# Rebuilding one of four attention stages of a vision tower: rotary attention with a transposed projection of image pairs

## The chip, the cores and the metric

One core of one Trainium2 chip (trn2). The metric is the device time of the kernel in microseconds (us), median of the runs; lower is better.

## The reference

The kernel is a small vision tower: a deformable-convolution tokenizer turns 32 images of 3x84x84 into 25 tokens of 192 numbers each, and four attention layers and four feed-forward layers follow, each with its residual and a layer norm behind it. The change touches the first attention layer alone. For x of 32 x 25 x 192 it computes

```python
# 12 heads of 16; LATENT = 32, so with n = 25 tokens ctx = n - LATENT = -7
ctx = n - LATENT
q, kv = _rope(_heads(x @ Wq)), _rope(_heads(x @ Wkv))     # kv serves as key and value
q = q * 16 ** (-0.5)
lkv, lkv_ctx = _ln(kv, ln_g, ln_b), _ln(kv[:, :ctx], ln_g, ln_b)   # layer norm of each head's 16 numbers
attn_lat = softmax(q[:, ctx:] @ kv.T)                    # the last 7 tokens attend to all 25
attn_ctx = softmax(q[:, :ctx] @ kv[:, :ctx].T)           # the first 18 only to the first 18
out_lat = _merge(attn_lat @ lkv) @ Wo_lat + bo_lat
out_ctx = _merge(attn_ctx @ lkv_ctx) @ Wo_ctx + bo_ctx
h = _layernorm(h + concatenate([out_ctx, out_lat], axis=1))
# _rope(t): t * cos(f) + concatenate([-t2, t1]) * sin(f), t1 and t2 the halves of a head's 16
```

## The kernel before

Tokens live in SBUF as `tw.y`, 8 tiles of 128 rows (TILES = 8). A tile holds 4 images (IMG_PER_TILE) of 25 tokens, each image padded to 32 rows (QUAD). The 12 heads go in 3 groups of 4 (GROUPS). The 192 features are contracted in two halves of 96 rows (HALVES, HALF). All is float32.

The program is a row of nine stages, one after the other: tokenizer, then attention and feed-forward of layers 0 to 3. Within a stage each engine has its own program, written out in the order in which it executes, and semaphores tie the engines together. No scheduler reorders anything. Stage 1, the rotary attention, is `softmax_attention` with kind "rope", opened by `AttentionBuffers`, whose block clears the buffers. It goes tile by tile in three steps of a software pipeline, `step(a, t, u, p)`: tile a is projected, tile t gets its scores, tile u is finished. On each engine:

- PE transposes the tokens (L258), projects q and kv of one tile token-major (L304: the transposed tokens are the stationary operand, 384 weight columns stream), transposes q and k head by head (L272, L274), makes the scores (L318), transposes the probabilities (L250), mixes the values (L287), transposes the result (L325) and multiplies it with both output matrices side by side (L332, 384 columns).
- DVE (VectorE) rotates (L349 to L352), centres kv and takes its variance (L355 to L360), scales it and applies the norm's gain and shift (L374 to L378), copies half of the keys (L431) and all values in 16 small copies (L440), divides by the softmax sum (L446, L448), adds the mask (L472), subtracts the maximum (L475, L477), and picks context or latent output row by row (L491, L494).
- ACT (ScalarE) copies transposed tiles out of PSUM, and makes Sqrt (L536) and Exp (L539) once per tile.
- POOL (GpSimd) adds the output bias (L552).

The layer norm is only begun here: `bn_stats` (L499) feeds a later part of the stage.

Two other attention stages, "unit" (stage 5) and "biased" (stage 7), already run through another function, `attention` (L557 on), which works on pairs of tiles. Its lines serve for comparison: it projects with the weights stationary and 200 token columns of two tiles streaming (L657), values as 64 small products per tile (L699), scores in 24 (L718), transposed probabilities (L727), the mix of the values (L739), the result transposed (L748), the output matrix in two halves (L756, L757); DVE spreads keys over four heads with a mask (L814), and divides (L859, L863). Stages 3 and 4 call the same pieces; L1298 is DVE's product of a projected bank of 400 columns with a table, in stage 3.

A float32 matmul of the code stands in the trace as two PE instructions, a transpose as one: the 12 products of L318 are the "x24" of a row.

## Time and profile before

| | us |
|---|---|
| median of 3 runs | 1305.06 (1305.06, 1314.97, 1294.93) |
| profiled execution, its own time | 1296.84 |
| its span | 1295.2 |
| PE busy in the span | 916.5 (71%) |
| DVE busy | 634.8 (49%) |
| ACT busy | 426.7 (33%) |
| stage 1, from the clearing of its buffers to the last of its `bn_stats` | 268.74 to 408.88 |

The profiled execution is the one whose rows are read below; its time lies 1.6 us above its span. A busy share is an average over nine stages with different limits, so the stage itself has to be read. Its three runs lie 20 us apart.

### The profile page before, as it was taken

To read this page: it belongs to the slowest core of one execution; us is meant where nothing else is said; L and a number is where in the kernel's file an instruction comes from. 1 tells how busy PE (TensorE), PEld (TensorE's weight loads), DVE (VectorE), ACT (ScalarE), POOL (GpSimd) and SP (SyncE) were. 2 spreads that over 40 slices of the span, in tenths; PEclk is the share of its full clock that TensorE was granted. 3 is DMA by queue.
4 is the path that set the end of the run, shared out by engine and by line. 5 is a ranking of instruction groups with operands and counts; after the bars stand their busy time and mean duration, and the time that the engine had idled before them with its cause. 6 is when DMAs were issued, how large, how long until landed. Compare 5 with 4: busy or idle time off the path is not lost. (4 is left out here: it accounts for less than half of the span.)

```text
span 1295.2 us, 25468 instructions
## 1 busy us (share of the span) xinstructions
PE 916.5 (71%) x9931; PEld 748.1 (58%) x9931; DVE 634.8 (49%) x1464; ACT 426.7 (33%) x728; POOL 214.8 (17%) x240
## 2 busy tenths in 40 slices
PE   4946677736766299358887658578778999386684
PEld 1336676423334199347776557366547999364573
DVE  1638899448774531365553225635281111246354
ACT  0148999123342112024443213334210112133132
POOL 2122232010000333142220010100002331200100
PEclk9969999855555599778998659868586999769598
DMA  4367787661000655100000060000053995100000
GB/s 126 80 135 182 191 205 196 175 156 25 0 0 1 217 142 129 60 1 2 2 2 1 2 163 4 2 2 3 2 133 80 238 258 124 32 2 3 1 4 20
DMA packets 63203, 100.35 MB, mean 77 GB/s; under 512 B 15812, under 2 KB 47096, under 8 KB 63104
## 3 DMA queue, kind: packets, MB, share of 16 engines
q1 hardware_dynamic: 57600, 93.25, 28.5%
q0 software_dynamic: 5504, 5.70, 2.1%
q8 instruction: 72, 1.18, 0.4%
q14 instruction: 27, 0.22, 0.1%
HBM read 91.34 MB, written 8.12 MB: 77 GB/s over the span
## 5 line engine op out<-in xcount | busy, mean ns | idle before, releaser
L1751 PE MATMUL ps_rows<-stage_strip,stage_hat_y 128*128 128x144 f32 x800 | 110.8, 295 | 53.2 <-ACT stage_hat_y L1718 53.2
L1751 PEld LDWEIGHTS ps_rows<-stage_strip,stage_hat_y 128*128 128x128 f32 x800 | 102.3, 193 | 61.8 <-ACT stage_hat_y L1718 36.5
L1782 DVE TENSOR_TENSOR stage_product<-ps_rows,stage_hat_x 128x1296 f32<-128x1296 f32 x80 | 68.7, 901 | 24.4 <-PE ps_rows L1751 23.7
L2558 DVE TENSOR_TENSOR L_ffnhid<-L_ffnact_gate,L_ffnbank_u 128x300 f32<-128x300 f32 x32 | 14.9, 467 | 119.0 <-ACT L_ffnact_gate L2576 119.0
L1790 DVE TENSOR_REDUCE stage_samples<-stage_product 128x1440 f32 x40 | 66.2, 1654 | 9.3 <-DVE stage_product L1782 9.3
L1733 POOL TENSOR_TENSOR stage_hat_x<-stage_pos_xT,stage_w_window_x 128x240 f32<-128x240 f32 x80 | 48.3, 625 | 108.7 <-DVE stage_product L1782 102.6
L1713 ACT ACTIVATE stage_hat_y<-stage_hat_y,stage_w_minus_row 80x1280 f32<-80x1280 f32 x40 | 54.4, 1361 | 26.9 <-DMA stage_hat_y<-places_y 26.4
L1556 PE MATMUL ps_conv<-stage_w_offset_w,stage_patches 128*100 128x512 f32 x96 | 44.0, 611 | 17.2 <-DMA stage_patches<-in_patchesT 17.2
L1718 ACT ACTIVATE stage_hat_y<-stage_hat_y 80x1280 f32<-80x1280 f32 x40 | 50.1, 1253 | 0.0
L1135 PE MATMUL L_attnbank_q<-L_attnhT,L_attnwq 97*128 97x200 f32 x192 | 43.2, 372 | 6.9 <-DVE L_attnqT L1298 6.7
L1135 PEld LDWEIGHTS L_attnbank_q<-L_attnhT,L_attnwq 97*128 97x128 f32 x192 | 36.7, 212 | 9.4 <-issue 8.7
L2522 PE MATMUL L_ffnbank_g<-L_ffnxT,L_ffn_win 96*128 96x100 f32 x240 | 41.0, 299 | 0.5 <-ACT L_ffnxT L2569 0.5
L2522 PE MATMUL L_ffnbank_u<-L_ffnxT,L_ffn_win 96*128 96x100 f32 x240 | 40.7, 297 | 0.0
L2491 POOL DMA_INDIRECT stage_y_rows<-L_ffndown,stage_choice_index x16 | 25.5, 1593 | 90.4 <-ACT L_ffndown L2583 90.4
L2576 ACT ACTIVATE L_ffnact_gate<-L_ffnbank_g 128x300 f32<-128x300 f32 x32 | 13.4, 420 | 80.5 <-PE L_ffnbank_u L2522 74.9
L1556 PEld LDWEIGHTS ps_conv<-stage_w_offset_w,stage_patches 128*100 128x100 f32 x96 | 16.0, 173 | 39.8 <-issue 22.6
L2342 DVE TENSOR_TENSOR L_ffnhid<-L_ffnact_gate,L_ffnbank_u 128x480 f32<-128x480 f32 x16 | 10.5, 654 | 55.6 <-ACT L_ffnact_gate L2366 50.4
L1174 PE MATMUL L_attnbank_o<-L_attnv_heads,L_attnwork 128*100 128x68 f32 x192 | 26.2, 314 | 16.1 <-ACT L_attnwork L1422 14.9
L2522 PEld LDWEIGHTS L_ffnbank_g<-L_ffnxT,L_ffn_win 96*128 96x128 f32 x240 | 36.0, 215 | 0.8 <-issue 0.8
L2522 PEld LDWEIGHTS L_ffnbank_u<-L_ffnxT,L_ffn_win 96*128 96x128 f32 x240 | 35.6, 213 | 0.0
L1174 PEld LDWEIGHTS L_attnbank_o<-L_attnv_heads,L_attnwork 128*100 128x100 f32 x192 | 25.0, 226 | 18.1 <-ACT L_attnwork L1422 16.0
L2290 PE MATMUL L_ffnbank_g<-L_ffnxT,L_ffn_win 96*128 96x240 f32 x128 | 33.0, 383 | 0.7 <-ACT L_ffnxT L2359 0.7
(430 smaller groups left out, 2197.6 us busy)
## 6 DMA issues: line engine op xcount, KB each, us to landing
stage_hat_y<-places_y SPq DMA_DIRECT2D x40, 400.0 KB
stage_strip<-in_strips SPq DMA_DIRECT2D x40, 315.0 KB
L_ffn_win<-in_L_ffn_Win SPq DMA_DIRECT2D x10, 1152.0 KB
stage_L_ffn_win<-in_L_ffn_Win SPq DMA_DIRECT2D x6, 1152.0 KB
L_ffnranks<-stage_ranks SPq DMA_DIRECT2D x16, 400.0 KB
L_ffn_win<-in_L_ffn_Win SPq DMA_DIRECT2D x8, 768.0 KB
L_ffn_wout<-in_L_ffn_Wout SPq DMA_DIRECT2D x10, 576.0 KB
stage_L_ffn_wout<-in_L_ffn_Wout SPq DMA_DIRECT2D x6, 576.0 KB
```

Of the source, the lines that this page charges most:

```text
L1135: mm = nc.tensor.matmul(bank_q[:, i * PAIR_TOKENS:(i + 1) * PAIR_TOKENS], wq[0:rows, k, c * GROUPS + g, :], tokens, start=(k == 0), stop=( ...
L1174: mm = nc.tensor.matmul(bank_o[0:QUERIES, j // 2, at:at + OUT_COLS], work[:, t % 2, j * GROUPS + g, :], v_heads[:, t % 4, j, g, :, :], sta ...
L1556: mm = nc.tensor.matmul(ps_conv[0:TILE_TOKENS, p, :], patches[:, p, c, :], w["offset_w"][:, c, :], start=(c == 0), stop=(c == SLABS - 1))
L1713: nc.scalar.activation(y, y, ACT.Abs, bias=w["minus_row"][0:ROWS_Y, :]).then_inc(s["hat_y_abs"], 1)
L1718: nc.scalar.activation(y, y, ACT.Relu, scale=-1.0, bias=1.0).then_inc(s["hat_y"], 1)
L1733: x = nc.gpsimd.tensor_tensor(hat_x[:, p, h * GRID * IMG_PER_TILE:(h + 1) * GRID * IMG_PER_TILE, :].rearrange("q (g j) x -> q g j x", j=IM ...
L1751: mm = nc.tensor.matmul(ps[:, p % 2, bank, at * cols:(at + 1) * cols], hat_y[:, p, g, h * P:(h + 1) * P], rhs.rearrange("q j c x -> q (j c ...
L1782: last = nc.vector.tensor_tensor(split(product[:, p % 2, slots.start * cols:slots.stop * cols]), ps[:, p % 2, banks, 0:used * cols].rearra ...
L1790: nc.vector.tensor_reduce(into.rearrange("q h c w -> q h w c"), by_window, AX_X, ALU.add).then_inc(s["summed"], 1)
L2290: mm = nc.tensor.matmul(ps[:, c, f, :], weights.win[e % NB][:, k, o:o + P], xT[:, e % 2, k, :], start=(k == 0), stop=(k == 1))
L2491: nc.gpsimd.indirect_dma_start(choice.y_rows, bass.IndirectOffsetOnAxis(choice.index[0:C, e:e + 1], 0), down[:, e % RING, :], None, bounds ...
L2522: mm = nc.tensor.matmul(ps[:, c, f, :], weights.win[e % NB][:, k, o:o + P], xT[:, e % 2, k, :], start=(k == 0), stop=(k == 1))
```

## The change

`AttentionBuffers` and `softmax_attention` go, `rope_attention` takes their place, with prepared weights: copies of Wq and Wkv whose two halves of each head are swapped, cos and sin tables by feature row, a centring matrix, the mask as two vectors whose outer product it is, and the output matrices with their biases as a 97th row. Apart from it, `build` and `layout` change only in what they load. The core of the diff:

```diff
-        w1 = halves("L0_attn_Wqkv", pending), halves("L0_attn_Wo", pending), tw.sb("w_L0_attn_bo", [P, DIM])
...
+        rope = {"qk": weight("w_L0_attn_qk", ins["L0_attn_qk"], [HALF, HALVES, 3, 2, P], pending),
+                "proj": weight("w_L0_attn_proj", ins["L0_attn_proj"], [PADDED_ROWS, 2, HALVES, DIM], pending),
+                "cos_sin": weight("w_rope_cos_sin", ins["rope_cos_sin"], [P, 2, TOKENS], pending), "centre": weight("w_rope_centre", ins["rope_centre"], [P, 4, 2 * HEAD_DIM], pending),
...
-            b = AttentionBuffers(tw)
-            softmax_attention(tw, b, "L0_attn", "rope", *w1, rope=rope, fetch=lambda sp: weights2.load(sp, range(4)))
+            rope_attention(tw, "L0_attn", rope, lambda sp: weights2.load(sp, range(4)))
```

PE's new functions (f counts pairs of tiles, t tiles; `bank_of` is bank_b for FIRST_K and LAST, bank_a for FIRST_Q):

```diff
+            def project(f, b):
+                pe.wait_ge(hT_ready, 2 * f + 2)
+                if b == LAST:
+                    pe.wait_ge(turned[FIRST_K], f + 1)
+                elif f:
+                    pe.wait_ge(turned[FIRST_Q if b == FIRST_Q else LAST], f)
+                for turn in range(2):
+                    for k in range(HALVES):
+                        tokens = hT[:, f % 2, k].rearrange("q z (j n) -> q (z j) n", n=QUAD)[:, :, 0:TOKENS]
+                        mm = nc.tensor.matmul(bank_of[b][:, turn * PAIR_TOKENS:(turn + 1) * PAIR_TOKENS], w["qk"][0:HALF, k, b, turn, :], tokens,
+                                              start=(k == 0), stop=(k == 1))
+                mm.then_inc(in_psum[b], 1)
+
+            def project_values(t):
+                f, z = t // 2, t % 2
+                pe.wait_ge(rotated[FIRST_K], f + 1)
+                pe.wait_ge(rotated[LAST], f + 1)
+                if t:
+                    pe.wait_ge(v_ready, t)
+                for j in range(IMG_PER_TILE):
+                    image = z * IMG_PER_TILE + j
+                    for a in range(4):
+                        to = ps_v[QUAD * a:QUAD * (a + 1), GROUPS * j:GROUPS * (j + 1), :].rearrange("n g d -> n (g d)")
+                        nc.tensor.matmul(to[:, 0:2 * HEAD_DIM], kr[:, f % 2, 0, image, :], w["centre"][:, a, :], start=True, stop=True)
+                        mm = nc.tensor.matmul(to[:, 2 * HEAD_DIM:], kr[half:P, f % 2, 1, image, :], w["centre"][half:P, a, HEAD_DIM:], start=True, stop=True)
+                mm.then_inc(v_in_psum, 1)
...
+                for g in range(GROUPS):
+                    rows = slice(half, P) if g == 1 else slice(0, half)
+                    nc.tensor.matmul(bank_s[:, g, 0:4 * TOKENS], w["context"][0:1, :], w["latent"][0:1, :], start=True, stop=False)
+                    for j in range(IMG_PER_TILE):
+                        mm = nc.tensor.matmul(bank_s[QUAD * j:QUAD * (j + 1), g, 0:4 * TOKENS], qT[rows, f % 2, g // 2, z * IMG_PER_TILE + j, :],
+                                              kd[rows, f % 2, g // 2, z * IMG_PER_TILE + j, :, :], start=False, stop=True)
...
+                for c in range(2):
+                    for k, rows in enumerate((HALF + 1, HALF)):
+                        mm = nc.tensor.matmul(ps_y, outT[0:rows, t % 2, c, k].rearrange("q j n -> q (j n)"), w["proj"][0:rows, c, k, :],
+                                              start=(c == 0 and k == 0), stop=(c == 1 and k == 1))
...
+            for i in range(-2, TILES + 2):
+                f, z = i // 2 + 1, i % 2
+                ahead = f < PAIRS
+                if 0 <= i < TILES:
+                    score(i)
+                if 1 <= i <= TILES:
+                    turn_probs(i - 1)
+                if ahead and z == 0:
+                    project(f, FIRST_K)
+                    project(f, FIRST_Q)
+                if 1 <= i <= TILES:
+                    mix_values(i - 1)
+                if i >= 2:
+                    turn_out(i - 2)
+                if ahead and z == 0:
+                    project(f, LAST)
+                if 0 <= i + 1 < TILES:
+                    project_values(i + 1)
+                if f + 1 < PAIRS:
+                    turn_tokens(2 * f + 2 + z)
+                if i >= 2:
+                    project_out(i - 2)
```

DVE's order, and its new pieces:

```diff
+            def turn(f, b):
...
+                nc.vector.tensor_tensor(pair(parts[:, f % 2, b].rearrange("p s n -> p (s n)")), pair(bank_of[b][:, 0:2 * PAIR_TOKENS]),
+                                        w["cos_sin"][:].unsqueeze(2).to_broadcast([P, 2, IMAGES_2, TOKENS]), ALU.mult).then_inc(turned[b], 1)
...
+            def store_values(t):
+                dve.wait_ge(v_inverse, t + 1)
...
+                for a in range(4):
+                    rows = slice(QUAD * a, QUAD * (a + 1))
+                    last = nc.vector.tensor_tensor(v_heads[rows, t % 4, :, :, a, 0:HEAD_DIM].rearrange("p j g d -> p (j g) d"), ps_v[rows],
+                                                   v_rstd[rows, t % 2, :].unsqueeze(2).to_broadcast([QUAD, IMG_PER_TILE * GROUPS, HEAD_DIM]), ALU.mult)
+                last.then_inc(v_ready, 1)
...
+            for i in range(-2, TILES + 2):
...
+                if 0 <= i < TILES:
+                    shift(i)
+                if 0 <= i < TILES:
+                    sum_values(i)
+                if 1 <= i <= TILES:
+                    divide(i - 1)
+                if ahead and z == 0:
+                    turn(f, FIRST_K)
+                    turn(f, FIRST_Q)
+                if ahead and z == 1:
+                    spread_last_keys(f)
...
+                    rows = w["proj"][0:HALF].rearrange("q c k n -> q (c k n)")
+                    nc.vector.tensor_scalar(rows, rows, w["gain"][:], None, ALU.mult).then_inc(scaled_out, 2)
+                if 0 <= i < TILES:
+                    store_values(i)
+                if ahead and z == 0:
+                    turn(f, LAST)
+                if i >= 2:
+                    add_residual(i - 2)
```

ACT makes the values' squares and their inverse deviation (Ln, then Exp), and POOL the sums of the two products of a rotation:

```diff
+                nc.scalar.activation(v_square[:], bank_h[:, 0:v_cols], ACT.Square).then_inc(v_squared, 1)
...
+                nc.scalar.activation(v_rstd[:, t % 2, :], v_rstd[:, t % 2, :], ACT.Ln, scale=1.0 / HEAD_DIM, bias=tw.eps[:]).then_inc(v_logged, 1)
+                act.wait_ge(v_logged, t + 1)
+                nc.scalar.activation(v_rstd[:, t % 2, :], v_rstd[:, t % 2, :], ACT.Exp, scale=-0.5).then_inc(v_inverse, 1)
...
+            for f in range(PAIRS):
+                pool.wait_ge(turned[FIRST_K], f + 1)
...
+                add(everything, kr, f, FIRST_K).then_inc(rotated[FIRST_K], 1)
...
+                add(everything, qT, f, FIRST_Q).then_inc(rotated[FIRST_Q], 1)
...
+                nc.gpsimd.tensor_tensor(kd[:, f % 2, 0], kr[:, f % 2, 0, :, 0:TOKENS].unsqueeze(2).to_broadcast(shape),
+                                        w["head_mask"][:].unsqueeze(1).unsqueeze(3).to_broadcast(shape), ALU.mult).then_inc(k_wide, 1)
...
+                add(low, qT, f, LAST).then_inc(last_q_rotated, 1)
...
+                add(high, kr, f, LAST).then_inc(rotated[LAST], 1)
```

What stands in a row now. PE, one step of the loop before (stage_probs of the tile being finished, stage_qk of the one in the middle):

```order
L250 MATMUL L_attnps_kT<-identity,stage_probs 128x128 x3
L258 MATMUL L_attnbank_h<-identity,stage_h 96x128 x2
L272 MATMUL L_attnps_qT<-identity,stage_qk 128x128 x3
L274 MATMUL L_attnps_kT<-identity,stage_qk 128x128 x3
L287 MATMUL L_attnps_o<-stage_v_heads,stage_pT 32x68 x12
L304 MATMUL L_attnps_qk<-w_L_attn_Wqkv,stage_hT 128x384 x2
L318 MATMUL L_attnps_s<-stage_kT,stage_qT 32x100 x12
L325 MATMUL L_attnbank_o<-identity,stage_out 96x128 x2
L332 MATMUL L_attnbank_v<-w_L_attn_Wo,stage_outT 128x384 x2
```

PE in the changed kernel, the even step i = 2, from its last group of scores on (bank_b twice: keys, then LAST; the pair L226, L227 stands 16 times, of which two are shown):

```order
L252 MATMUL L_attnbank_t<-identity,L_attnprobs 128x128 x3
L212 MATMUL L_attnbank_b<-L_attnhT,w_L_attn_qk 128x200 x4
L212 MATMUL L_attnbank_a<-L_attnhT,w_L_attn_qk 128x200 x4
L263 MATMUL L_attnbank_o<-L_attnv_heads,L_attnpT 32x68 x12
L272 MATMUL L_attnbank_t<-identity,L_attnout 96x128 x2
L212 MATMUL L_attnbank_b<-L_attnhT,w_L_attn_qk 128x200 x4
L226 MATMUL L_attnbank_h<-w_rope_centre,L_attnkr 32x32
L227 MATMUL L_attnbank_h<-w_rope_centre,L_attnkr 32x16
L226 MATMUL L_attnbank_h<-w_rope_centre,L_attnkr 32x32
L227 MATMUL L_attnbank_h<-w_rope_centre,L_attnkr 32x16
```

The six transposes of queries and keys are gone, the projection comes once for two tiles, and 32 small products for the values are new. In an odd step the three rows of L212 are absent, so the values' products come right behind L263 and L272.

DVE in the changed kernel, the odd step i = 3:

```order
L366 TENSOR_REDUCE L_attntop<-L_attnbank_s 128x12
L370 TENSOR_TENSOR L_attnprobs<-L_attnbank_s,L_attntop 128x12x25
L344 TENSOR_REDUCE L_attnv_rstd<-L_attnv_square 128x12
L375 RECIPROCAL L_attninv_sum<-L_attnbank_o 128x12
L379 TENSOR_TENSOR L_attnout<-L_attnbank_o,L_attninv_sum 128x192
L337 TENSOR_TENSOR L_attnkd<-L_attnkr,w_rope_head_mask 64x800
L353 TENSOR_TENSOR L_attnv_heads<-L_attnbank_h,L_attnv_rstd 32x12x16 x4
L384 TENSOR_TENSOR y<-L_attnbank_o,y 128x192
L386 BN_STATS moments<-y 128x6
```

`store_values` (L353) stands behind `divide` and `spread_last_keys` (L337), and the values' products of the next tile, on PE, wait for it.

## Rows read from the trace of the kernel before

**Rows 1.** Windows: stages 1, 5, 7: busy PE, PEld, DVE, ACT, POOL, PEclk, DMA, GB/s.

```profile
267.20:411.35 144.15, 85.24 (x552) 47.12 (x552) 99.29 (x344) 44.13 (x80) 8.20 (x10) 0.55 0.13 33
833.10:925.70 92.60, 65.22 (x1056) 51.22 (x1056) 44.30 (x108) 29.75 (x75) 10.81 (x8) 0.65 0.01 2
1126.60:1196.60 70.00, 49.68 (x1032) 39.02 (x1032) 38.77 (x93) 22.71 (x55) 4.67 (x4) 0.77 0.01 2
```

**Rows 2.** Timeline of stage 1: its clearing, first scores and last operation.

```profile
268.74 1.46 POOL L191 MEMSET stage_v_heads<- 128x1632 f32 x1 [30.09 <-POOLq L83]
...
290.37 0.72 PE L318 MATMUL L_attnps_s<-stage_kT,stage_qT 128*32 128x100 f32 x24
...
408.52 0.36 DVE L499 BATCH_NORM_STATS2 moments<-y 128x6 f32<-128x192 f32 x1
```

**Rows 3.** Costliest DVE group of stage 1, by shape.

```profile
L440 DVE COPY stage_v_heads<-stage_v 32x48 f32<-32x48 f32 x128 | 23.5, 183 | 1.9
```

**Rows 4.** Windows: three pair periods and the tail of the unit stage.

```profile
856.70:872.70 16.00, 12.42 (x225) 10.30 (x226) 7.27 (x17) 5.62 (x15) 1.53 (x1) 0.68 0.01 2
872.70:887.70 15.00, 12.37 (x269) 10.25 (x270) 8.58 (x22) 6.70 (x18) 1.54 (x1) 0.88 0.01 3
887.70:904.00 16.30, 13.34 (x264) 10.78 (x265) 8.61 (x22) 6.02 (x17) 1.53 (x1) 0.80 0.01 2
904.00:923.80 19.80, 15.17 (x153) 10.11 (x153) 7.07 (x20) 3.67 (x10) 0.00 (x0) 0.51 0.00 1
```

**Rows 5.** Timeline of the unit stage at half clock: PE, and DVE's reciprocal.

```profile
857.53 1.70 PE L657 MATMUL L_attnbank_b<-L_attnhT,w_L_attn_qk 97*128 97x200 f32 x4
...
861.83 1.59 PE L699 MATMUL L_attnbank_h<-w_L_attn_v,L_attnhT 97*32 97x51 f32 x64
...
887.67 0.89 PE L718 MATMUL L_attnbank_s<-L_attnkd,L_attnqT 64*32 64x100 f32 x24 [1.54 <-DVE L_attnkd L814]
888.49 0.90 PE L727 MATMUL L_attnbank_t<-identity,L_attnprobs 128*128 128x128 f32 x3
...
893.32 0.91 PE L739 MATMUL L_attnbank_o<-L_attnv_heads,L_attnpT 128*32 128x68 f32 x24
894.30 0.23 DVE L859 RECIPROCAL L_attninv_sum<-L_attnbank_o 128x12 f32<-128x12 f32 x1 [4.71 <-PE L_attnbank_o L739]
...
907.88 1.01 PE L756 MATMUL L_attnbank_o<-w_L_attn_proj,L_attnoutT 97*128 97x192 f32 x2 [0.46 <-ACT L_attnoutT L959]
908.69 0.85 PE L757 MATMUL L_attnbank_o<-w_L_attn_proj,L_attnoutT 96*128 96x192 f32 x2
```

**Rows 6.** The same at full clock, with ACT's copy of the probabilities.

```profile
895.41 0.59 PE L756 MATMUL L_attnbank_o<-w_L_attn_proj,L_attnoutT 97*128 97x192 f32 x2
...
896.26 0.55 PE L718 MATMUL L_attnbank_s<-L_attnkd,L_attnqT 64*32 64x100 f32 x24
896.74 0.55 PE L727 MATMUL L_attnbank_t<-identity,L_attnprobs 128*128 128x128 f32 x3
897.12 0.84 PE L683 MATMUL L_attnbank_h<-L_attnsquare,w_same_head 128*128 128x200 f32 x4
897.33 0.48 ACT L952 COPY L_attnpT<-L_attnbank_t 128x384 f32<-128x384 f32 x1 [1.11 <-PE L_attnbank_t L727]
898.24 0.56 PE L739 MATMUL L_attnbank_o<-L_attnv_heads,L_attnpT 128*32 128x68 f32 x24
898.87 0.23 DVE L859 RECIPROCAL L_attninv_sum<-L_attnbank_o 128x12 f32<-128x12 f32 x1 [0.87 <-PE L_attnbank_o L739]
```

**Rows 7.** Source lines: min/median/max ns of one, from first to last, shapes.

```profile
L1298 DVE TENSOR_TENSOR L_attnqT<-L_attnbank_q,w_cheb_q x24: 567/574/578, 571.1 to 695.8; 128x400 f32<-128x400 f32 x24
L814 DVE TENSOR_TENSOR L_attnkd<-L_attnk_unit,w_head_mask x4: 1366/1368/1375, 855.2 to 902.5; 64x800 f32<-64x800 f32 x4
L552 POOL TENSOR_TENSOR stage_resid<-stage_h,w_L_attn_bo x8: 587/588/592, 276.1 to 390.3; 128x192 f32<-128x192 f32 x8
L863 DVE TENSOR_TENSOR L_attnout<-L_attnbank_o,L_attninv_sum x16: 356/357/358, 867.9 to 1190.7; 128x192 f32<-128x192 f32 x16
```

More of the change, by code:

```diff
@@ L542, in _, with store_tokens, square_values @@
-            tiles(act, step)
+            def store_tokens(t):
+                act.wait_ge(hT_in_psum, t + 1)
+                f, z = t // 2, t % 2
+                if f >= 2:
+                    act.wait_ge(in_psum[LAST], f - 1)
+                    act.wait_ge(in_psum[FIRST_Q], f - 1)
+                nc.scalar.copy(hT[:, f % 2, :, z, :], ps_hT.rearrange("q (k n) -> q k n", n=P)).then_inc(hT_ready, 1)
+            def square_values(t):
+                act.wait_ge(v_in_psum, t + 1)
+                if t:
+                    act.wait_ge(v_summed, t)
+                nc.scalar.activation(v_square[:], bank_h[:, 0:v_cols], ACT.Square).then_inc(v_squared, 1)
@@ new lines, in store_probs, with store_out @@
+            def store_probs(t):
+                act.wait_ge(pT_in_psum, t + 1)
+                if t >= 2:
+                    act.wait_ge(out_in_psum, t - 1)
+                nc.scalar.copy(pT[:, t % 2].rearrange("p g n -> p (g n)"), bank_t[:, 0:GROUPS * P]).then_inc(pT_ready, 1)
+            def store_out(t):
+                act.wait_ge(outT_in_psum, t + 1)
+                act.wait_ge(ones_ready, 1)
+                if t >= 2:
+                    act.wait_ge(y_in_psum, t - 1)
+                for c, kind in enumerate(KINDS):
+                    last = nc.scalar.copy(outT[0:HALF, t % 2, c, :, :, kind], ps_outT.rearrange("q (k j n) -> q k j n", k=HALVES, n=QUAD)[:, :, :, kind])
+                last.then_inc(outT_ready, 1)
@@ new lines, in _ @@
+            nc.scalar.preload_act_table_set("natural_log_exp_and_others")
+            store_tokens(0)
+            store_tokens(1)
+            for i in range(-2, TILES + 2):
+                f, z = i // 2 + 1, i % 2
+                if 0 <= i < TILES:
+                    square_values(i)
+                if 1 <= i <= TILES:
+                    store_probs(i - 1)
+                if 0 <= i < TILES:
+                    exponent(i)
+                    invert_values(i)
+                if i >= 2:
+                    store_out(i - 2)
+                if f + 1 < PAIRS:
+                    store_tokens(2 * f + 2 + z)
@@ L544, in _ @@
         @block.gpsimd
         def _(pool):
[L546 to L554 removed]
+            nc.gpsimd.memset(outT[:], 0.0).then_inc(out_cleared, 1)
+            nc.gpsimd.memset(kr[:], 0.0).then_inc(qk_cleared, 1)
@@ new lines, in _, with add @@
+            nc.gpsimd.memset(qT[:], 0.0).then_inc(qk_cleared, 1)
+            nc.gpsimd.memset(probs[:], 0.0).then_inc(probs_cleared, 1)
+            nc.gpsimd.memset(v_heads[:], 0.0).then_inc(v_cleared, 1)
+            pool.wait_ge(qk_cleared, 2)
+            def add(rows, to, f, b):
+                p = parts[rows, f % 2, b]
+                return nc.gpsimd.tensor_tensor(to[rows, f % 2, b // 2, :, 0:TOKENS], by_image(p[:, 0, :]), by_image(p[:, 1, :]), ALU.add)
+            everything, low, high = slice(0, P), slice(0, half), slice(half, P)
@@ L2970, in with_bias @@
         return np.stack([np.concatenate([weight[:HALF], ends[0]]), np.concatenate([weight[HALF:], ends[1]])], 1)
+    o["L0_attn_proj"] = np.stack([with_bias(a[x], a[y]) for x, y in rope_proj], 1)
     def heads_first(x):
```

587 lines of the change are left out of this document (207 added, 380 removed).

## The prediction

> **What bounds the kernel now.** I first read the busy time by stage [rows 1]. In stage 1 (first row, 144.15 us with the norm behind it) VectorE, DVE, is busy 99.29 us in 344 operations and PE 85.24 us: neither is full, and they take turns. The other two rows are attention stages of the same size whose program resembles the new one. They take 92.60 and 70.00 us, with DVE busy 44.30 and 38.77 us. So the old stage is long because of DVE's many operations. The largest group of them is the 128 small value copies, 23.5 us [rows 3].
>
> The timeline shows what can be won [rows 2]: clearing begins at 268.74, the first scores start at 290.37 and the last statistics at 408.52. That is 118.15 us for eight tiles, 14.8 us each; a part of it is the drain behind the last scores. I count a pair of tiles as 30.8 us before. Nothing outside this stretch changes but weight loads, which come long before their use and lie beside the tokenizer's 268 us; I count them at nothing. If they were late the stage would start later, by microseconds, which the range holds.
>
> The last thing to see is the granted TensorE clock: 0.55 in the old stage, 0.65 and 0.77 in the other two [rows 1]. The clock has two levels, 2.4 GHz (1.0) and 1.2 GHz (0.5). Within the unit stage it is 0.68, 0.88 and 0.80 in three pair periods and 0.51 in the tail [rows 4]. Every PE duration therefore needs two prices.
>
> **The prices.** At half clock [rows 5]: twelve instructions of 200 columns fill 857.53 to 861.83, 0.36 us each; 24 score instructions 0.82 (887.67 to 888.49); two output instructions of 192 columns 0.81 (907.88 to 908.69); from mix to DVE's reciprocal 0.98; 64 value instructions 1.59. At full clock [rows 6]: scores 0.48, probability transposes 0.38, output instructions 0.85 for four, mix to reciprocal 0.63. From the transposes' start to the mix it is 1.17: 0.59 until ACT's copy starts, its 0.48 and 0.1 of hand-over; at half clock 0.3 more. 200 columns at full clock: half of 0.36, 0.18. DVE and POOL [rows 7]: a product of 128x400 is 0.57, 64x800 1.37, 128x192 out of PSUM 0.36, a POOL addition of 192 columns 0.59.
>
> **Part by part.**
>
> *The vanishing work.* Rotation, centring, variance, gain, shift, mask, key and value copies go from DVE. New on DVE per pair: three products of 128x400 (1.7), one 64x800 (1.37), and per tile four stores of 32x192 (I take 0.39 each, the 128x192 row and a little, so as if the price went by columns alone; the 0.183 of a 32x48 copy [rows 3] bounds it below), a sum and a subtraction of the maximum as before. That makes some 11 us per pair, 45 us in all against 99. DVE no longer bounds. What is late next is the chain through PE, DVE and back, so I lay out the two steps.
>
> *Even step, full / half clock.* Scores 0.48 / 0.82 with three mask products, six instructions of 100 columns at 0.11 / 0.22 (half of the 200-column price and 0.02 to 0.04 for the change of weights): 1.15 / 2.15. Transposes 0.38 / 0.69. Keys and queries, 16 instructions: 2.88 / 5.73. Mix to divide 0.63 / 0.98. So far 5.04 / 9.55. Now PE's value products wait for `store_values`, and on DVE stand before it: divide 0.63, two products 0.6 each, then the stores 1.56, hand-over 0.1: 3.5. PE fills this with LAST, which itself waits for divide and the keys' product (1.23) and takes 8 instructions, 1.44 / 2.87, so at half clock it ends at 4.1 and sets the time. Then values 1.1 / 2.0 (32 products in 64 instructions; the row of 64 at half clock has 51 columns each, here 32 and 16, but two different stationaries in a row, so I add a quarter), token transposes 0.3 / 0.45, output 8 instructions 1.72 / 3.2. Sum **11.65 / 19.3**.
>
> *Odd step.* 1.15 / 2.15, transposes to mix 1.17 / 1.46, mix to divide 0.63 / 0.98: 2.95 / 4.6. Before `store_values` stand divide 0.63 and the spread of the last keys 1.41; with the stores and hand-over 3.7, and PE has only two transposes to do meanwhile: a wait of over 3 us. Then 3.1 / 5.65. Sum **9.75 / 13.95**. A pair: **21.4 / 33.25**. As a fixed part and one that goes with the clock c: 9.55 + 11.85/c.
>
> *Waits added.* Queued behind `project_values` on PE are the token transposes and `project_out`; behind those, the next scores. POOL's work per pair is four additions of 0.6 and the wide product of 1.53 [rows 4], 3.9 us in a pair of over 20. The last addition comes some 1.3 us after DVE's product of LAST, before the even step's output products end. I count it at nothing; if that cover is gone it costs 1 us a pair. DVE's `spread_last_keys` waits for the same addition. The mask costs PE 0.66 / 1.32 a tile and saves DVE an addition that is no longer on the chain: by itself a loss, and in the sum. The second output matrix (8 instructions in place of 4 wider ones) likewise. The two small ACT operations on the values' deviation lie beside DVE's division and products.
>
> *Does this method hold?* The same layout for the unit stage gives 13.2 / 20.7 a pair, or 5.7 + 7.5/c. At its clocks [rows 4] that is 16.7, 14.2 and 15.1, together 46.0, where the trace has 47.3 (16.00, 15.00, 16.30). It is 3% short.
>
> *The start.* Clearing still begins at 268.74, with twice the value buffer on POOL (1.46 before [rows 2]), but the keys' buffer comes before it. I estimate two token tiles and their copies at 3 us, bias products 2 to 3 (8 instructions of 192 columns and the first transposes), keys, queries and LAST 24 instructions at 0.18 to 0.36, then additions of 0.6, first values and key spread, with gain and bias folded in on DVE: first scores at 286.6, against 290.37. The bounds are 283 and 291.
>
> *The sum.* The first pair (16.0 / 23.95) lacks its predecessors' two outputs (1.72 each at full clock) and, in its even step, their transposes, mix and division (1.64): 8.05 + 7.95/c. Two full pairs. Tiles 6 and 7 and the drain, without projections and with one value group: 10.65 + 11.05/c. What clock? PE's work per time is like the unit stage's in the even step (0.79 mean in its pairs), but the odd step has the hole of 3 us; the old stage, full of holes, had 0.55. I take 0.72, and 0.58 in the tail, a little over the 0.51 that the unit stage's tail had [rows 4]. 286.6 + 19.1 + 52.0 + 29.7 = 387.4, against 408.9. **Saved: 21.5 us.** The profiled execution had 1296.84, so one like it takes 1275.3. Its time is 8 us under the median of the runs; I take the saving off the median: 1305.06 - 21.5 = 1283.6, **1284 us**.
>
> **A price with no row.** For each tile the values alternate 16 times between a product of 128 rows (L226) and one of the lower 64 rows (L227) in the same 32 output rows. No row shows such a change of height. The nearest are L699's 64 instructions, 0.025 us each at half clock [rows 5], and the scores, which change between upper and lower 64 rows twice, at no visible cost [rows 6]. So the bounds are 0.9 us a tile and whatever a fully serial pair costs: a full-height instruction takes 0.4 us for 192 columns at half clock; with fill and drain for 16 to 32 columns I estimate up to 0.12 us each, 7.7 us a tile. I take 2.0 at half clock, near L699.
>
> The Trainium skill, "TensorEngine Tiling (Array Packing)", section "Key Properties", says that changing the tiling mode drains the engine. By that rule each of these 32 products would wait for the one before, and the result would be the fourth case below; the traces shown here neither confirm nor exclude it.
>
> **The rivals.**
> A. As above. Its own range is a saving of 10 to 30, by the start's bounds (+3.6, -4.4), a clock 0.08 off either way (6 us) and the 3% of the method.
> B. The clock stays higher, because PE's work is denser than in the old stage. At 0.85 throughout: 286.6 + 17.4 + 47.0 + 23.65 = 374.7, 34 saved, 1271 us. At full clock the end is 367.1, 42 saved, 1263 us; with values and mask at their lower bounds 1254. For it: 0.88 in one pair period [rows 4], 0.77 in stage 7. Against: the hole of the odd step.
> C. The clock stays near half throughout, as in the old stage: 286.6 + 23.95 + 66.5 + 32.75 = 409.8. Nothing saved, 1306 us. The DVE work that went is replaced by PE columns at half speed.
> D, the slower side. The alternation of heights serialises the value products, and they lie on PE's chain with nothing beside them. At 8 us per tile more, 6 over the 2.0 counted, 48 us come on top of A: 27 us slower, 1332 us. It decides from 21.5/8 = 2.7 us more per tile, or 0.07 us per instruction. Against it: no small product in the trace shows such a price.
>
> **How the numbers follow.** A 0.52, B 0.28, C 0.13, D 0.07. The likeliest is A: 1284. The range reaches over B to near its full-clock end and over C: 1258 to 1310, leaving out D, the edge of B and of C. About 2% (26 us) is what a measurement can tell from no change here, as the three runs lie 20 us apart. Faster by over 2% (below 1279) is nearly all of B and a sixth of A: 0.36. Slower by over 2% (above 1331) is over half of D: 0.04. Within: 0.60.
>
> **What would show it.** In the changed profile: first scores at 286.6, last `bn_stats` near 387, a period of 26 us per pair; DVE busy about 50 us in the stage, PE the busiest engine; granted clock near 0.7; in odd steps a PE wait of over 3 us that DVE's store of the values (L353) ends; L226 and L227 together 1.1 to 2.0 us a tile. The step most likely to be wrong is the clock, then the price of the values. I would be wrong on the mechanism if the odd steps' wait is ended by POOL, if L226 to L227 takes over 4 us, or if stages that the change doesn't touch move by more than 10 us.

## The result: slower, and where the profile after puts it

The changed kernel takes 1339.12 us (median of 4 runs, 1335.5 to 1346.53), the kernel before 1306.05 (4 runs, 1294.93 to 1314.97): a ratio of 1.029, 95% interval 1.0201 to 1.0378. It is slower by some 33 to 38 us, not faster by 21. The profiled execution took 1342.13, its span is 1340.5. Ratios here and below come from the undisturbed executions of both kernels in one series of runs alone, so they can differ a little from the quotient of the medians.

First the stretch that answers to the first row of [rows 1], cut in the same way around the stage (columns as there):

```profile
277.90:456.60 178.70, 151.89 (x1168) 114.78 (x1168) 44.18 (x122) 21.06 (x67) 21.88 (x25) 0.60 0.12 27
```

DVE has lost what the prediction said it would: 44.18 us busy in place of 99.29. The clock is higher, 0.60 for 0.55. But PE is busy 151.89 us in place of 85.24. The timeline of the stage, to be laid beside [rows 2]:

```profile
279.42 0.63 PE L200 MATMUL L_attnbank_a<-identity,y 128*96 128x128 f32 x2 [1.98 <-PEq L83]
...
303.01 0.56 PE L243 MATMUL L_attnbank_s<-L_attnkd,L_attnqT 64*32 64x100 f32 x8
...
453.80 0.36 DVE L386 BATCH_NORM_STATS2 moments<-y 128x6 f32<-128x192 f32 x1
```

The stage runs from 279.42 to 454.16: **174.7 us**, where it had 140.1 (268.74 to 408.88). (Before, the first token transposes came 7.4 us behind the start of the clearing, at 276.12; here the clearing and they start together, so both lengths count from the start of the clearing.) That is 34.6 us, as much as lies between the two medians. Behind the stage the two profiles are equal: 1340.5 - 454.16 and 1295.2 - 408.88 are both 886.3 us. The stage also begins 10.7 us later here; the start moves by about as much between series of runs (last experiment). From here on I give for every kernel its time and the length of this stage, from the first token transposes to the last `bn_stats`; two profiles of the changed kernel gave 174.7 and 174.8 us.

PE's costliest groups of the stage, by shape (busy time, mean ns, idle before):

```profile
L226 PE MATMUL L_attnbank_h<-w_rope_centre,L_attnkr 128*32 128x32 f32 x256 | 37.6, 237 | 14.3 <-DVE L_attnv_heads L353 11.7 <-POOL L_attnkr L486 2.5
L227 PE MATMUL L_attnbank_h<-w_rope_centre,L_attnkr 64*32 64x16 f32 x256 | 34.8, 213 | 0.0
L212 PE MATMUL L_attnbank_b<-L_attnhT,w_L_attn_qk 96*128 96x200 f32 x64 | 18.4, 448 | 1.9 <-DVE L_attnparts L329 1.9
L241 PE MATMUL L_attnbank_s<-w_rope_latent,w_rope_context 1*128 1x100 f32 x48 | 17.8, 473 | 0.0
L243 PE MATMUL L_attnbank_s<-L_attnkd,L_attnqT 64*32 64x100 f32 x192 | 13.4, 372 | 0.0
```

The two value groups hold the engine for 72.4 us, and the mask's 48 instructions for 17.8, more than the 192 of the scores. How one tile's values run at half clock, at full clock, and how its scores run, is in the timeline:

```profile
294.42 0.29 PE L226 MATMUL L_attnbank_h<-w_rope_centre,L_attnkr 128*32 128x32 f32 x2 [2.53 <-POOL L_attnkr L486]
294.63 0.29 PE L227 MATMUL L_attnbank_h<-w_rope_centre,L_attnkr 64*32 64x16 f32 x2
294.85 0.31 PE L226 MATMUL L_attnbank_h<-w_rope_centre,L_attnkr 128*32 128x32 f32 x2
...
301.53 0.29 PE L227 MATMUL L_attnbank_h<-w_rope_centre,L_attnkr 64*32 64x16 f32 x2
301.75 0.66 PE L200 MATMUL L_attnbank_a<-identity,y 128*96 128x128 f32 x2
302.34 0.74 PE L241 MATMUL L_attnbank_s<-w_rope_latent,w_rope_context 1*128 1x100 f32 x2
...
303.50 0.74 PE L241 MATMUL L_attnbank_s<-w_rope_latent,w_rope_context 1*128 1x100 f32 x2
304.18 0.56 PE L243 MATMUL L_attnbank_s<-L_attnkd,L_attnqT 64*32 64x100 f32 x8
304.66 0.74 PE L241 MATMUL L_attnbank_s<-w_rope_latent,w_rope_context 1*128 1x100 f32 x2
305.33 0.56 PE L243 MATMUL L_attnbank_s<-L_attnkd,L_attnqT 64*32 64x100 f32 x8
305.82 3.03 PE L212 MATMUL L_attnbank_b<-L_attnhT,w_L_attn_qk 96*128 96x200 f32 x8
...
329.00 0.29 PE L226 MATMUL L_attnbank_h<-w_rope_centre,L_attnkr 128*32 128x32 f32 x2 [3.35 <-DVE L_attnv_heads L353]
...
394.12 0.25 PE L226 MATMUL L_attnbank_h<-w_rope_centre,L_attnkr 128*32 128x32 f32 x2
394.29 0.23 PE L227 MATMUL L_attnbank_h<-w_rope_centre,L_attnkr 64*32 64x16 f32 x2
394.46 0.25 PE L226 MATMUL L_attnbank_h<-w_rope_centre,L_attnkr 128*32 128x32 f32 x2
```

A row of the values holds two instructions (one product), because the next product is of another line: the list alternates to the end. A pair of products takes 0.46 us at half clock (the average to 301.75: 7.33 us for 16 pairs) and 0.34 at full (394.12 to 394.46), where 64 instructions of L699 took 1.59 at half [rows 5]. Added over the eight groups, in part at full clock, this is 54.4 us. The scores with their masks take 3.48 us (302.34 to 305.82), where 24 score instructions alone take 0.82 [rows 5]. The wait for DVE's stores ahead of an odd step's values, 3.35 us, is there as forecast.

### The profile page after: what moved, and what is told of

It is laid out like the page before. It is cut to its first block and busy times, and to the rows that moved or that the text cites. A ratio compares the mean times of both kernels' runs of the same rounds, so it can differ in the third digit from the quotient of the medians.

```text
span 1340.5 us, 26268 instructions
## 1 busy us (share of the span) xinstructions
PE 984.2 (73%) x10547; PEld 816.6 (61%) x10547; DVE 580.9 (43%) x1242; ACT 404.0 (30%) x715; POOL 228.5 (17%) x255
## 5 line engine op out<-in xcount | busy, mean ns | idle before, releaser
L1735 DVE TENSOR_TENSOR stage_product<-ps_rows,stage_hat_x 128x1296 f32<-128x1296 f32 x80 | 68.8, 902 | 34.8 <-PE ps_rows L1704 34.6
L226 PE MATMUL L_attnbank_h<-w_rope_centre,L_attnkr 128*32 128x32 f32 x256 | 37.6, 237 | 14.3 <-DVE L_attnv_heads L353 11.7
L227 PE MATMUL L_attnbank_h<-w_rope_centre,L_attnkr 64*32 64x16 f32 x256 | 34.8, 213 | 0.0
```

What stands on the lines that cost most here:

```text
L226: nc.tensor.matmul(to[:, 0:2 * HEAD_DIM], kr[:, f % 2, 0, image, :], w["centre"][:, a, :], start=True, stop=True)
L227: mm = nc.tensor.matmul(to[:, 2 * HEAD_DIM:], kr[half:P, f % 2, 1, image, :], w["centre"][half:P, a, HEAD_DIM:], start=True, stop=True)
L1735: last = nc.vector.tensor_tensor(split(product[:, p % 2, slots.start * cols:slots.stop * cols]), ps[:, p % 2, banks, 0:used * cols].rearra ...
```

## The experiments

The experiments ran in three series, with the kernel before again in each: its medians were 1298.42 us in the first (the next four experiments), 1295.87 in the second (both, mask on DVE, stores first, one output) and 1304.10 in the third (the rest). So times of different series are best compared by their ratios to it, or by the stage. One profile of each kernel was read.

The height of a product is the number of rows that it reads, its width the number of output rows that it writes (its stationary operand has that many rows and columns: 64*32 in a row of PE is 64 high and 32 wide). Three theories of the values' price stood at first. H: PE waits whenever the height of its products changes, here between 128 and 64 rows. S: two products in a row into the same 32 output rows wait for each other. B: products this small cost that much whatever stands beside them.

**Grouped.** All 16 products of L226, then all 16 of L227.

```diff
+                def to(j, a):
+                    return ps_v[QUAD * a:QUAD * (a + 1), GROUPS * j:GROUPS * (j + 1), :].rearrange("n g d -> n (g d)")
+
                 for j in range(IMG_PER_TILE):
-                    image = z * IMG_PER_TILE + j
                     for a in range(4):
-                        to = ps_v[QUAD * a:QUAD * (a + 1), GROUPS * j:GROUPS * (j + 1), :].rearrange("n g d -> n (g d)")
-                        nc.tensor.matmul(to[:, 0:2 * HEAD_DIM], kr[:, f % 2, 0, image, :], w["centre"][:, a, :], start=True, stop=True)
-                        mm = nc.tensor.matmul(to[:, 2 * HEAD_DIM:], kr[half:P, f % 2, 1, image, :], w["centre"][half:P, a, HEAD_DIM:], start=True, stop=True)
+                        nc.tensor.matmul(to(j, a)[:, 0:2 * HEAD_DIM], kr[:, f % 2, 0, z * IMG_PER_TILE + j, :], w["centre"][:, a, :], start=True, stop=True)
+                for j in range(IMG_PER_TILE):
+                    for a in range(4):
+                        mm = nc.tensor.matmul(to(j, a)[:, 2 * HEAD_DIM:], kr[half:P, f % 2, 1, z * IMG_PER_TILE + j, :], w["centre"][half:P, a, HEAD_DIM:], start=True, stop=True)
```

> The 32 value products of a tile in another order: all 16 of L226 (128 rows), then all 16 of L227 (64 rows). In the changed kernel a group of them takes 7.3 us at half clock and 5.4 at full, 0.115 and 0.085 us per instruction. Theory H (height): every change between 128 and 64 rows waits for the product before; with one change in place of 31 the group falls to 1.3 to 2.5 us and the kernel to 1295 to 1300 us. Theory S (strip): two products in a row into the same 32 output rows wait for each other; here neighbours lie in different strips, so the same as H. Theory B (a product this small costs 0.115 us whatever its neighbours): nothing changes, 1339 us.

Measured: 1280.66 us (1279.24 to 1284.53), 0.9885 of the kernel before (0.9847 to 0.9922); the stage 124.6 us, 50 less. The same 64 instructions, at half clock (L227 and L230 are the changed kernel's L226 and L227):

```profile
356.27 0.66 PE L227 MATMUL L_attnbank_h<-w_rope_centre,L_attnkr 128*32 128x32 f32 x32 [2.99 <-DVE L_attnv_heads L356]
356.86 0.63 PE L230 MATMUL L_attnbank_h<-w_rope_centre,L_attnkr 64*32 64x16 f32 x32
357.42 2.93 PE L287 MATMUL L_attnbank_o<-w_L_attn_proj,L_attnoutT 97*128 97x192 f32 x8
```

1.15 us in place of 7.33, at the same clock and with not one instruction less. The 32 instructions of 64 rows take 0.56 of it (356.86 to 357.42), so being lower does not cost by itself. B is out. The kernel came out faster than the 1295 to 1300 us that H had given. Part of that is the series, in which the kernel before was 8 us quicker too; and the groups shrank below my lower bound of 1.3 us. The ratio's interval lies below 1, but the gain is under 2%.

**Next strip.** Heights still alternate, but neighbours write different strips.

```diff
...
+                        b = (a + 1) % 4
...
+                        mm = nc.tensor.matmul(to(j, b)[:, 2 * HEAD_DIM:], kr[half:P, f % 2, 1, z * IMG_PER_TILE + j, :], w["centre"][half:P, b, HEAD_DIM:], start=True, stop=True)
```

> The heights still alternate, 128, 64, 128, 64, but the 64-row product goes into the next strip of 32 output rows, not into the one just written. H: unchanged, 7.3 us a group at half clock and 1339 us. S: the group falls below 2.5 us and the kernel to 1295 to 1300 us. B: unchanged.

Measured: 1329.99 us (1321.63 to 1336.15), ratio 1.026 (1.0198 to 1.0323); the stage 177.3 us; the two value groups of the stage busy 37.2 and 34.5 us, where the changed kernel has 37.6 and 34.8. S is out. (The stage is 2.5 us longer than the changed kernel's, which I can't explain; differences of this size between single profiles carry little by themselves.)

**Full height.** L227 reads all 128 rows; order and strips stay.

```diff
-                        mm = nc.tensor.matmul(to[:, 2 * HEAD_DIM:], kr[half:P, f % 2, 1, image, :], w["centre"][half:P, a, HEAD_DIM:], start=True, stop=True)
+                        mm = nc.tensor.matmul(to[:, 2 * HEAD_DIM:], kr[:, f % 2, 1, image, :], w["centre"][:, a, HEAD_DIM:], start=True, stop=True)
```

> L227 reads all 128 rows in place of the lower 64 (the upper rows of these keys are zero, so the sum is the same); order and strips as in the changed kernel. H: no change of height is left, the group falls to 1.3 to 2.5 us, 1295 to 1300 us. S: unchanged, 1339 us. B: unchanged.

Measured: 1283.9 us (1266.72 to 1294.69, 10 runs), ratio 0.9854 (0.9797 to 0.991); the stage 121.0 us.

```profile
352.78 0.33 PE L226 MATMUL L_attnbank_h<-w_rope_centre,L_attnkr 128*32 128x32 f32 x6 [2.87 <-DVE L_attnv_heads L353]
352.88 0.21 PE L227 MATMUL L_attnbank_h<-w_rope_centre,L_attnkr 128*32 128x16 f32 x1
...
353.81 2.80 PE L284 MATMUL L_attnbank_o<-w_L_attn_proj,L_attnoutT 97*128 97x192 f32 x8
```

And the window of its stage (columns as in [rows 1]):

```profile
263.00:388.00 125.00, 97.49 (x1168) 75.90 (x1168) 44.22 (x122) 21.58 (x67) 21.91 (x25) 0.65 0.16 39
```

The group takes 1.03 us (352.78 to 353.81), although every product now reads as much or more and the order is that of the changed kernel. (Its rows are short and overlap: products of one shape run into each other.) H holds: a pair costs 0.46 us with two changes of height and 0.064 without, so 0.2 us a change at half clock. At full clock a pair costs 0.34 with two changes and 0.046 without (this trace's group from 343.43 to 344.16, by 16), so 0.15 each. PE is busy 97.49 us in the stage, at a clock of 0.65.

**Mask first.** The mask product has 1 row and 128 output rows, the score products 64 and 32. The values stay as in the changed kernel; the three masks stand together.

```diff
                 for g in range(GROUPS):
-                    rows = slice(half, P) if g == 1 else slice(0, half)
                     nc.tensor.matmul(bank_s[:, g, 0:4 * TOKENS], w["context"][0:1, :], w["latent"][0:1, :], start=True, stop=False)
+                for g in range(GROUPS):
+                    rows = slice(half, P) if g == 1 else slice(0, half)
```

> The values as in the changed kernel; the three mask products (L241, 1 row, 128 output rows) stand together ahead of the 12 score products (L243, 64 rows, 32 output rows) in place of one ahead of each four. A group of scores takes 3.5 us at half clock now, 1.16 for each mask with its four products. H: five changes of shape become one; if each costs what it costs among the values, about 0.1 to 0.2 us, the group falls to 2.5 to 2.9 us, and the kernel by 5 to 8 us to 1332. S and B: the group stays at 3.5 us, 1339 us.

Measured: 1329.88 us (1323.56 to 1347.92), ratio 1.025 (1.019 to 1.031); the stage 168.8 us, 5.9 less than the changed kernel's, within the 5 to 8 us of H. At half clock:

```profile
360.98 1.60 PE L240 MATMUL L_attnbank_s<-w_rope_latent,w_rope_context 1*128 1x100 f32 x6
362.51 0.89 PE L244 MATMUL L_attnbank_s<-L_attnkd,L_attnqT 64*32 64x100 f32 x24
363.33 0.90 PE L253 MATMUL L_attnbank_t<-identity,L_attnprobs 128*128 128x128 f32 x3
```

2.35 us in place of 3.48: 1.13 for four changes inside the group less, some 0.28 each. (All eight groups ran at half clock here and in the changed kernel: 9.0 us less in all, of which the stage's length shows 5.9.) The scores are back at 0.82, and the six mask instructions cost 1.53, most of what is left, one change of shape included.

**Both.** Full height and mask first.

> Full-height values and the three mask products together ahead of the scores. The first run of either kind took stage 1 from 174.7 us to 121.0 and to 168.8. Theory H (each change of tile shape on PE costs about 0.2 us, wherever it stands) makes the two add: stage 1 at 121.0 - 5.9 = 115, the kernel 5 to 6 us below the full-height one, 1278. Rival (PE's chain isn't the bound once the values are short; the wait for DVE's stores takes back what the scores give): stage 1 within 2 us of 121, 1284 us.

Measured: 1273.24 us (1267.68 to 1282.57), ratio 0.9839 (0.9784 to 0.9894); the stage 117.1 us. 3.9 us under full height alone, between the theory's 5.9 and the rival's 2. The groups of scores with masks took 15.7 us over the stage, where full height had 20.9, so 5.2 less; the clock was nearly the same (0.65 and 0.66), so a part of the gain does not come through. At full clock such a group took 1.31 us here and 2.09 there: 0.2 for each of the four changes.

**Mask on DVE.** Full height, and the mask an addition on DVE again (0.47 us, a third pass over the scores); PE waits for it before the next scores.

```diff
-                    nc.tensor.matmul(bank_s[:, g, 0:4 * TOKENS], w["context"][0:1, :], w["latent"][0:1, :], start=True, stop=False)
...
+                nc.vector.tensor_tensor(scores, bank_s[:, :, 0:4 * TOKENS].rearrange("p g (a n) -> p g a n", n=TOKENS),
+                                        w["mask"][:].unsqueeze(1).unsqueeze(1).to_broadcast([P, GROUPS, 4, TOKENS]), ALU.add).then_inc(masked, 1)
```

> Full-height values, and the mask as an addition on DVE, as before the change, in place of the three products. PE's group of scores falls from 3.5 to 0.82 us at half clock and from 2.1 to 0.48 at full. If the mask product is a loss because PE is the chain here: eight tiles by 1.6 to 2.7 us, 13 to 20 us off stage 1, 101 to 108 us in place of 121, kernel 1265 to 1271. If DVE's addition (0.47 us) and its later release of the scores' bank take its place on the chain: 4 us more per eight tiles come back, 105 to 112. If the clock falls as PE gets idler, less: 112 to 118.

Measured: 1262.69 us (1258.46 to 1266.63), ratio 0.9749 (0.9706 to 0.9793); the stage 102.1 us, 18.9 less than full height alone, within the 101 to 108 of the first answer.

```profile
291.40 0.55 PE L243 MATMUL L_attnbank_s<-L_attnkd,L_attnqT 64*32 64x100 f32 x24
291.88 0.55 PE L252 MATMUL L_attnbank_t<-identity,L_attnprobs 128*128 128x128 f32 x3
```

The scores are one group of 24 again, 0.48 us at full clock. Their groups took 5.2 us over the stage in place of 20.9, which is 15.7 of the 18.9; the rest was not traced (the clock was 0.68 for 0.66), and DVE's addition of 0.47 us a tile does not show in the length. As a product the mask cost 2.4 us a tile, 2.0 of it in its own groups.

**Stores first.** On top of that, in odd steps `spread_last_keys` behind `store_values`.

```diff
-                if ahead and z == 1:
-                    spread_last_keys(f)
...
                 if 0 <= i < TILES:
                     store_values(i)
+                if ahead and z == 1:
+                    spread_last_keys(f)
```

> As the one before, and in odd steps DVE's spread of the last keys (0.99 us) stands behind the stores of the values, for which PE waits 2.9 us there. If that wait is on the chain: 0.99 us by three odd steps with a pair ahead, 3 us off stage 1. If ACT's Ln and Exp or POOL's sums end the wait next, or the next scores then wait for the keys: less than 1 us.

Measured: 1258.63 us (1256.42 to 1267.61), ratio 0.9732 (0.9683 to 0.9781); the stage 98.2 us, 3.9 less, where 3 were expected. The values of the same tile, with PE's wait for the stores ahead of them, without this edit, with it, and with the next one (three traces):

```profile
296.95 0.33 PE L227 MATMUL L_attnbank_h<-w_rope_centre,L_attnkr 128*32 128x32 f32 x4 [3.39 <-DVE L_attnv_heads L353]
...
297.31 0.33 PE L227 MATMUL L_attnbank_h<-w_rope_centre,L_attnkr 128*32 128x32 f32 x4 [2.50 <-DVE L_attnv_heads L353]
...
303.31 0.23 PE L227 MATMUL L_attnbank_h<-w_rope_centre,L_attnkr 128*32 128x32 f32 x3 [1.83 <-DVE L_attnv_heads L353]
```

The waits of the three odd steps with a pair ahead shrank by 0.9 us each, 2.7 of the 3.9: the wait was on the chain. By the times alone the gain is not told from none, since the two ratios' intervals overlap.

**Sums early.** The same, and `sum_values` ahead of `shift`, ACT's inverse ahead of the exponent, stores ahead of the division in odd steps.

> The kernel with the stores first; DVE sums the values' squares before it touches the scores, ACT inverts before the exponent, and in odd steps the stores come before the division. If PE's wait for the stores (3 us in an odd step) is DVE's own order: 0.6 us by four odd steps, 2 to 3 us off stage 1's 98.2. If ACT's chain from the sum to the inverse (0.5 us and the copy of the probabilities ahead of it) ends the wait: nothing, or 1 to 2 us more in even steps, where the exponent comes later.

Measured: 1255.65 us (1247.67 to 1267.42), ratio 0.9696 (0.9599 to 0.9794) in another series of runs; the stage 96.8 us, 1.5 less. The length lies between the two answers. The waits say more: those of the three odd steps fell from 2.5, 2.3 and 2.3 us to 1.8, 1.5 and 1.5, so there DVE's own order had held the stores, as the first answer had it; the first even step's wait grew from 0.4 to 1.0, which gives part of it back.

**One output.** Full height, without the latent output matrix.

```diff
-                for c in range(2):
+                for c in range(1):
```

> Full-height values, and the product with the latent output matrix left out (the last 7 tokens get no output): 4 PE instructions in place of 8 per tile. It prices the second matrix. The prediction's 0.40 us per instruction at half clock and 0.215 at full gives 0.9 to 1.6 us a tile, 9 to 12 us off stage 1's 121. If the products lie beside a wait, under 4 us.

Measured: 1280.54 us (1272.65 to 1291.46), ratio 0.9894 (0.983 to 0.9958); the stage 113.2 us, 7.8 less than 121.0, a little under the 9 expected. The clock was 0.62 where full height had 0.66, which takes back a part: the scores with masks, which the edit leaves alone, took 23.6 us over the stage, for 20.9.

**Width, between and behind.** Is it the height alone? Two kernels on the one with the stores first add 16 idle products per tile with a stationary of 128 columns; all products read 128 rows. One puts an idle product behind each pair, the other all behind the 32 (there in a loop of their own).

```diff
+                        mm = nc.tensor.matmul(bank_h[:, 256:256 + HEAD_DIM], tw.identity[:], w["centre"][:, a, 0:HEAD_DIM], start=True, stop=True)
```

> The kernel with the stores first and, in each tile's values, 16 idle products more (128 rows, a stationary of 128 columns, 16 columns streamed, into unused columns of the bank), one behind each pair of 32-wide products. All products read 128 rows, so only the width of the output changes, 32 to 128 and back, 32 times a tile. Theory W (a change of width costs what a change of height costs): 0.1 to 0.2 us by 32 by 8, 25 to 50 us more in stage 1 than the next kernel, which has the same products with one change. Theory R (only the height matters): the two are within 4 us.

> The same 16 idle products, all behind the 32. Both theories: their own price alone, 32 instructions at the 0.1 to 0.23 us that a transpose of this size takes, 3.5 to 6.5 us a tile, stage 1 at 98 + 28 to 52, 126 to 150 us.

Measured: between, 1359.19 us (1352.98 to 1374.14), ratio 1.0522 (1.0445 to 1.06), the stage 203.7 us; behind, 1314.94 (1306.98 to 1321.26), ratio 1.019 (1.0084 to 1.0296), the stage 152.5, a little over the 150 given. The medians differ by 44 us, the stages by 51, of which the groups with the values are 49 (103.3 and 54.2 us). (The first one's profiled execution, 1374.14, is its longest, so its stage may be a little long; the clock in the stage was 0.57 and 0.59.) Between, first at half clock (0.50 in a window on these rows), then at full (1.00):

```profile
299.94 0.61 PE L229 MATMUL L_attnbank_h<-w_rope_centre,identity 128*128 128x16 f32 x2
300.48 0.32 PE L227 MATMUL L_attnbank_h<-w_rope_centre,L_attnkr 128*32 128x32 f32 x2
300.61 0.27 PE L228 MATMUL L_attnbank_h<-w_rope_centre,L_attnkr 128*32 128x16 f32 x2
300.81 0.61 PE L229 MATMUL L_attnbank_h<-w_rope_centre,identity 128*128 128x16 f32 x2
...
313.80 0.39 PE L229 MATMUL L_attnbank_h<-w_rope_centre,identity 128*128 128x16 f32 x2
...
314.91 0.40 PE L229 MATMUL L_attnbank_h<-w_rope_centre,identity 128*128 128x16 f32 x2
```

and behind, at half clock (0.50):

```profile
292.61 7.01 PE L231 MATMUL L_attnbank_h<-w_rope_centre,identity 128*128 128x16 f32 x32
299.46 0.64 PE L201 MATMUL L_attnbank_a<-identity,y 128*96 128x128 f32 x2
```

At half clock a round of three products takes 0.87 us between. The idle product alone takes 0.43 (6.85 by 16), the pair 0.064. So two changes of width cost 0.38 us, 0.19 each. At full clock the round takes 0.555 (two from 313.80 to 314.91), the idle product 0.224 (in the other trace 16 of them fill 337.72 to 341.31, 3.59 us), the pair 0.046: 0.14 a change. Theory W holds: a change of width costs what one of height costs, 0.2 and 0.15.

**The changed kernel again.**

> The changed kernel itself, again. In its first profile stage 1 began 11 us later than before (279.4 against 268.7), though the tokenizer's code is the same; in eight other profiles it began at 264 to 268. If that was chance: it begins below 272, stage 1 takes 174 to 177 us, and the span is 1325 to 1335. If the changed weights' loads delay the tokenizer: it begins near 279 again.

Measured: 1333.31 us (1321.88 to 1337.88), ratio 1.0314 (1.0199 to 1.043); the stage 174.8 us, to 0.1 that of the first profile. It began at 273.06, above the 272 that I had set. But the three other kernels of that series began at 274.6 to 277.0, with the same loads as the two kernels with the mask on DVE that began at 264 to 266 in the series before. So the start moves with the series of runs (each on another chip), and the loads alone don't set it. What does set it stays open: the loads were not varied by themselves, and this kernel's two starts are among the later ones.

## Why the prediction was wrong

**The bound, and what goes from DVE: right.** DVE 44.2 us for a forecast 45 to 50. The key spread took 0.99 us, not 1.37, and the stores 1.46 a tile for 1.56.

**The layout of the steps: right, once two prices are put in.** Full height shows it. Its stage took 121.0 us at a clock of 0.66, where the forecast end of 387.4 gives 118.7 at 0.72 and 0.58. The sum at 0.66, with this kernel's 7.4 us for the values and 20.9 for the scores with masks over eight tiles in place of its own 12.5 and 13.3, gives 122.8. First scores came 17.6 us after the start (282.10 - 264.52), forecast 17.9 (286.6 - 268.74). The odd step's wait that DVE's stores end is there, 3.35 us in the changed kernel, and POOL never ended it but at the start. A slip in the sum is small: the first pair's own terms leave 16.3 at full clock, where it has 16.0.

**The step that failed: the price with no row.** I took 2.0 us at half clock and 1.1 at full for a tile's values, near L699. They took 7.33 and 5.5, 54.4 us over eight tiles where the sum has about 12: 42 us. That is also the sign of a wrong mechanism that I had named, over 4 us. The bounds that I worked out, 0.9 to 7.7 us, held it; I chose a value near the lower end because L699 and the scores were the nearest rows. But neither of them changes shape: L699's 64 instructions are all 97 or 96 rows by 32, and the scores go between the upper and the lower 64 rows at the same height. They are alike in size, not in the one respect that decided. The fourth case, D, had the mechanism and nearly the time, 1332 us against 1339, and I gave it 0.07. Its time is near partly by luck: it had 48 us for the values, where they cost 42, and nothing for the mask. Range and sign failed with that choice.

The rule in the Trainium skill ("TensorEngine Tiling (Array Packing)", section "Key Properties"), that changing the tiling mode drains the engine, was cited and then outweighed. The runs agree with it: 0.2 us a change of height and 0.19 of width at half clock, 0.15 and 0.14 at full, and none that shows for a change of place at one shape (strips of full height 0.064 us a pair; 24 score instructions, which change between the upper and lower 64 rows, 0.82).

**A second term, the mask, was mis-sized.** 2.15 us at half clock for scores with masks; they take 3.48, 27.8 us over eight tiles (all eight ran at half clock) for about 13 in the sum: 15 us. I had allowed 0.02 to 0.04 us for the change of weights and overlooked that each mask is 1 row by 128 between products of 64 by 32: the same mechanism, five more times a tile. I also wrote that as a product it was a loss by itself, of 0.66 to 1.32 us a tile; taken back to DVE it gave 18.9 us, 2.4 a tile.

**The account:** 118.7 + 42 + 15 = 175.7 us, for 174.7 measured. That it closes so well is partly luck: the clock was 0.60 where the sum has 0.72 and 0.58, and with 0.60 throughout the same working gives some 181 us.

**Untouched stages: right.** Behind the stage both profiles have 886.3 us. That they agree to the tenth is chance: in the profiles of the experiments this rest lies between 883.7 and 894.9 us.

What stays open: whether a change of both height and width, as with the mask, costs one wait or two. Its 0.28 us at half clock and 0.2 at full lie between one (0.2 and 0.15) and two.

## What to carry to other kernels

Products of the same shape (rows read, output rows) flow into each other on PE; a change of shape stops the flow. Before many small products are interleaved, list the shapes in PE's order: grouping them, or reading idle rows to keep the height, turned the change from 3% slower into 1.2 to 1.5% faster than before (a gain under the 2% that counts as clear here), with no instruction less. Work moved from an idle DVE onto PE's chain, as the mask was, is paid there: with the mask back on DVE and the stores first, the kernel stands at 0.973 of the one before.

When a term has no row, the nearest row is the one that shares the suspected mechanism, not the size; if no row does, the upper bound deserves a real chance in the forecast.

## What the runs showed of the hardware

A product that reads 1 row was not cheap for it. With 128 output rows and 100 columns, six instructions took 1.53 us at half clock, one change of shape included: 0.21 to 0.26 each. The idle products, 128 rows by 128 output rows with 16 columns, took 0.21 each, and 96 rows by 128 with 200 columns 0.36.

A store of 32x192 on DVE out of PSUM took 0.353 us, where 128x192 took 0.357 [rows 7]: at the same 192 columns, a quarter of the rows cost the same. A 64x800 product took 0.99 us here and 1.37 in the unit stage [rows 7]; why was not tested.

The clock in this stage was 0.60 with PE busy 151.9 of 178.7 us, and 0.65 with PE busy 97.5 of 125.0: the longer busy time did not go with the higher level more often. Why was not tested.

In the stage before, ACT has an ACT_TABLE_LOAD beside nearly every Sqrt (L536) and Exp (L539), seven of each, 1.28 us long:

```profile
353.25 1.28 ACT L536 ACT_TABLE_LOAD   x1
...
356.19 1.28 ACT L539 ACT_TABLE_LOAD   x1
```

That is 18.0 us of its 42.6 busy ones. The changed stage, with Square, Ln and Exp, has one such load. The prediction doesn't price this, and no run takes it apart from the rest of the change.
